# Fourteen expert tiles inside the last fourteen attention groups of a fused attention and mixture-of-experts block

## What is computed

```python
x = x + layernorm(attention(layernorm(x)))         # 16 heads of 16, causal, f16 weights
x = x + layernorm(moe(layernorm(x)))
...
logits = xt @ Ws + bs                              # 8 experts, two are taken for each row
topk_w, topk_idx = top_k(logits, 2); topk_w = softmax(topk_w)
h = silu(xt @ Wg[e]) * (xt @ Wu[e])                # F = 688
out = sum over the two experts e of topk_w * (h @ Wd[e])
```

## Time and profile before

| | us |
|---|---|
| median of 3 runs | 1003.47 (1001.80 to 1004.06) |
| profiled execution | 1003.02 |
| its span | 1001.3 |
| TensorE, VectorE, ScalarE, GpSimd busy | 824.3, 670.9, 549.9, 414.9 |
| TensorE clock granted, mean | 0.699 |

### The profile page before, as it was taken

The page is one execution under the profiler, slowest core; times in us unless marked ns, Lnnn a source line. Parts: engine busy times, 40 slices in busy tenths (PEclk is TensorE's granted clock), DMA queues, the critical chain, the costliest instruction groups (busy, mean ns, idle before and its releaser), DMA issues. The chain is left out here.

```text
span 1001.3 us, 22338 instructions
## 1 busy us (share of the span) xinstructions
PE 824.3 (82%) x6606; PEld 472.7 (47%) x6607; DVE 670.9 (67%) x2625; ACT 549.9 (55%) x1007; POOL 414.9 (41%) x428
## 2 busy tenths in 40 slices
PE   3488787799999999999982099999999999999800
PEld 1122232233333333333331087877877877877600
DVE  5667788888888988888864345555555555555535
ACT  4588877665565565556561044555555455455325
POOL 3565645562534534253445322333323323333316
PEclk9555555555555555555555599999999999999955
DMA  5344232228000101000011242323323323233164
GB/s 160 117 126 129 88 112 65 70 79 301 29 27 23 33 17 38 2 17 27 15 30 33 79 112 39 47 36 43 43 36 47 42 37 47 37 42 47 22 199 147
DMA packets 69219, 66.17 MB, mean 66 GB/s; under 512 B 5536, under 2 KB 62752, under 8 KB 69152
## 3 DMA queue, kind: packets, MB, share of 16 engines
q1 hardware_dynamic: 55872, 50.86, 16.7%
q0 software_dynamic: 13280, 14.49, 10.6%
HBM read 34.04 MB, written 31.29 MB: 65 GB/s over the span
## 5 line engine op out<-in xcount | busy, mean ns | idle before, releaser
L580 ACT ACTIVATE pT<-bank 128x512 f16<-128x512 f32 (+1 forms) x384 | 200.4, 530 | 161.9 <-PE bank L949 160.0
L691 DVE CUSTOM_DVE_ANT_0 unused<-bank,mask 128x384 f16<-128x384 f32 (+3 forms) x512 | 234.6, 483 | 73.9 <-PE bank L940 71.4
L1231 POOL DMA_INDIRECT expert_rows<-y_sb,dest x78 | 121.5, 1558 | 263.4 <-DVE y_sb L1350 224.1
L949 PE MATMUL bank<-qT,kT 32*128 32x384 f16 (+3 forms) x512 | 203.0, 449 | 23.8 <-ACT pT L580 23.6
L940 PE MATMUL bank<-kT,qT 32*128 32x384 f16 (+3 forms) x512 | 201.0, 446 | 16.8 <-DVE nmax L691 15.9
L1390 PE MATMUL bank<-xT,gu_part 128*128 128x256 f16 (+1 forms) x1716 | 202.7, 276 | 4.8 <-issue 3.8
L1390 PEld LDWEIGHTS bank<-xT,gu_part 128*128 (+1 forms) x1716 | 168.7, 100 | 36.8 <-issue 7.7
L1415 PE MATMUL bank<-wd_part,h 128*128 (+2 forms) x1326 | 163.6, 273 | 1.2 <-ACT h L1268 0.2
L482 POOL TENSOR_SCALAR_AFFINE_SELECT pT<-pT 128x512 f16<-128x512 f16 x128 | 79.8, 635 | 155.6 <-ACT pT L580 155.1
L1415 PEld LDWEIGHTS bank<-wd_part,h 128*128 128x128 f16 (+2 forms) x1326 | 117.2, 97 | 37.5 <-issue 24.5
L1268 ACT ACTIVATE h<-hid 128x512 f16<-128x512 f32 (+2 forms) x156 | 81.7, 523 | 89.0 <-DVE hid L1330 86.6
(11 more groups left out here) (150 smaller groups left out, 925.9 us busy)
## 6 DMA issues: line engine op xcount, KB each, us to landing
expert_rows<-clear SPq DMA_DIRECT2D x1, 8192.0 KB, 26.8
stage<-wg SPq DMA_DIRECT2D x8, 688.0 KB, 4.0
stage<-wu SPq DMA_DIRECT2D x8, 688.0 KB, 4.1
stage<-wd SPq DMA_DIRECT2D x8, 640.0 KB, 4.3
xin<-dispatch_rows SPq DMA_DIRECT2D x39, 130.0 KB
ys<-expert_rows SPq DMA_DIRECT2D x16, 256.0 KB, 6.0
out<-res SPq DMA_DIRECT2D x16, 256.0 KB, 2.1
x_sb<-x SPq DMA_DIRECT2D x8, 256.0 KB
```

The lines of the kernel that those rows point to most:

```text
L580: sc.activation(pT[:, lo:hi], ST_BANK[i % 2][:, 0:hi - lo], ACT.Exp, scale=1.0 / INV_SCALE).then_inc(p_ready, 1)
L691: last = v.tensor_tensor_reduce(out=unused[:, i % 2, at:at + n], in0=S_BANK[i % 2][:, at:at + n], in1=mask[:, T - n:T], scale=-1.0, scalar ...
L949: last = mm(ST_BANK[i % 2][:, at:at + n], kT[32 * j:32 * j + 32, g, P * kt:P * (kt + 1)], qT[32 * j:32 * j + 32, g, P * kt:T], start=True, ...
L1231: gp.indirect_dma_start(out=ys_dram[:, :], in_=y_sb[j][:, t, :], in_offset=None, out_offset=bass.IndirectOffsetOnAxis(ap=dest[j][:, t:t + ...
```

## The change

Fourteen of the 39 tiles (`EARLY_TILES`) are worked on inside groups 18 to 31 (`FIRST_TILE = 18`); `experts` keeps 25 (`LATER_TILES`). In each of these groups:

- TensorE does one of six chunks of gate and up products in each even step (`tile_up`, 8 products, the last chunk 4), one of six down chunks in steps 7, 9 and 11 and, for the tile of the group before, in steps 1, 3 and 5 (`tile_down`, 6 products, the last chunk 4), and transposes the next tile's rows in step 6. The gate and up chunk stands in one PSUM bank (`X_BANK`, the former `K_BANK`), gate in one half and up in the other, so `tile_up` waits for `hid_ready` of the chunk before. The down sums stand in the former `M_BANK`. All projections and transposes of attention share the remaining bank, one every second step.
- ScalarE takes tanh of half the gate in the even steps (`tanh`), makes high parts (`tile_high`) and takes the tile's result with the row's share (`take_tile_y`).
- VectorE computes silu times up in two operations at each odd step (`gate` and, at the step's end, `product`), and subtracts the low parts at fixed steps (`tile_low` at 6, 10, 11; `tile_last_low` at step 1 of the next group).
- GpSimd copies the rows' numbers and shares (`take_tile`) and issues the stores (`store_tile`, after the first cut of the next group; the last one after the last group).
- From sequence 3 on, VectorE plans which full tiles exist (`plan`, 17 small operations a sequence); SyncE loads them one group ahead.

Throughout attention `norm_centre` is gone: `norm_scale` subtracts the mean and multiplies in one operation, with the mean copied to f32 by GpSimd in `rsqrt`; the copies of y out of PSUM go from VectorE to ScalarE (`evict`); `x1` shares `y`'s memory. The table in `experts` starts each expert after the rows already done.

```diff
+FIRST_TILE = 4 * G + 2
+EARLY_TILES = G * B - FIRST_TILE
+LATER_TILES = TILES - EARLY_TILES
+CP = FC // 2
...
-        AT_Q, AT_K, AT_V, AT_MAXIMA = (1, 2), (3, 4), 5, (6, 7)
-        AT_ATT_T, AT_NEXT_T, AT_Y, AT_XN2_T = ((0, 7), (0, 8)), ((0, 10), (0, 11)), ((1, 0), (1, 2)), (2, 11)
-        AT_LOGITS, AT_RANKS = (3, 1), (3, 8)
+        EARLY_AT = ({"q": (1, 2), "k": (3, 4), "v": (5,), "max": (6, 7), "attT": (7, 8), "xnT": (10, 11)},
...
+                    {"q": (1, 2), "k": (3, 4), "v": (5,), "max": (6, 7), "logits": (1,), "ranks": (8,)})
+        TILE_AT = ({"q": (1,), "k": (3,), "v": (5,), "max": (7,), "attT": (9,), "xnT": (11,)},
...
+                   {"logits": (1,), "q": (3,), "k": (5,), "max": (7,), "ranks": (9,), "v": (11,)})
+        AT_TILE_T = 6
+        AT_UP = {2 * c: c for c in range(FC)}
+        AT_DOWN, AT_LATE_DOWN = {7: 0, 9: 1, 11: 2}, {1: 3, 3: 4, 5: 5}
...
+        HOME = {"q": 0, "max": 0, "k": 1, "y0": 1, "logits": 1, "ranks": 1, "v": 2, "attT": 2, "xnT": 2, "y1": 2,
+                "xn2T": 2}
+        TAIL_HOME = {"attT": 0, "y0": 1, "y1": 0, "xn2T": 0, "logits": 1, "ranks": 1}
...
+                def load_tile(n):
+                    sp.wait_ge(plan_ready, PLAN_OF[n] + 1)
+                    sp.wait_ge(keep["scattered"], 16 * TOP * QT * (PLAN_OF[n] + 2))
+                    if n:
+                        sp.wait_ge(tile_xT_mm, n)
+                        sp.wait_ge(tile_taken, n)
+                    else:
+                        sp.wait_ge(keep["cleared"], 16)
+                    row = sp.value_load(table[0:1, 0, n:n + 1], min_val=0, max_val=ROWS - TS)
+                    sp.dma_start(xin[:, :, :], xs_dram[bass.ds(row, TS), :].rearrange("(t p) d -> p t d", p=P)
+                                 ).then_inc(tile_in, 16)
...
                     gp.tensor_scalar(veps[:, :], mv[:, :, 1], LN_EPS16, None, ALU.add).then_inc(veps_ready, 1)
+                    gp.tensor_copy(mean[:, :], mv[:, :, 0]).then_inc(mean_ready, 1)
...
+                def take_tile(n):
+                    pool.wait_ge(tile_in, 16 * n + 16)
+                    if n >= 2:
+                        pool.wait_ge(tile_y_ready, n - 1)
+                        pool.wait_ge(keep["ys_early"], 32 * (n - 1))
+                    gp.tensor_copy(dest[n % 2][:, :], xin[:, :, :].bitcast(U32)[:, :, D // 2])
+                    gp.tensor_scalar(share[n % 2][:, :], xin[:, :, D // 2 + 1], 1.0 / (WSCALE * HSCALE), None, ALU.mult
+                                     ).then_inc(tile_taken, 1)
...
+                def store_tile(n):
+                    pool.wait_ge(tile_y_ready, n + 1)
+                    if n:
+                        pool.wait_ge(keep["ys_early"], 32 * n)
+                    else:
+                        pool.wait_ge(keep["cleared"], 16)
+                    for t in range(TS // P):
+                        gp.indirect_dma_start(
+                            out=ys_dram[:, :], in_=y_sb[:, t, :], in_offset=None,
+                            out_offset=bass.IndirectOffsetOnAxis(ap=dest[n % 2][:, t:t + 1], axis=0),
+                            compute_op=ALU.add,
+                        ).then_inc(keep["ys_early"], 16)
...
+                            if n >= 1 and c == 0:
+                                store_tile(n - 1)
+                            if n >= -1 and n + 1 < EARLY_TILES and c == 1:
+                                take_tile(n + 1)
...
+                store_tile(EARLY_TILES - 1)
...
+                def tanh(n, c):
+                    rows, cols = slice(0, P if c < FC - 1 else FR), slice(TS * (c % 2), TS * (c % 2) + TS)
+                    act.wait_ge(up_mm, FC * n + c + 1)
+                    if n == 0 and c == 0:
+                        act.wait_ge(lo_ready, PIECES)
+                    if n and c < FC - 1:
+                        act.wait_ge(h2_ready, CP * (n - 1) + c // 2 + 1)
+                    if n and c == FC - 1:
+                        act.wait_ge(low_ready, n)
+                    sc.activation(hid[rows, c // 2, cols], X_BANK[rows, 0:TS], ACT.Tanh, scale=0.5 / WSCALE
+                                  ).then_inc(tanh_ready, 1)
...
+                def tile_high(n, part):
+                    if n == 0 and part == 0:
+                        act.wait_ge(rows_cleared, 1)
+                    act.wait_ge(hid_ready, FC * n + (2, 4, 5, 6)[part])
+                    if n:
+                        act.wait_ge(down_mm, CP * (n - 1) + min(part, CP - 1) + 1)
+                    rows, m, cols = ((slice(0, P), 0, slice(0, 2 * TS)), (slice(0, P), 1, slice(0, 2 * TS)),
+                                     (slice(0, P), 2, slice(0, TS)), (slice(0, FR), 2, slice(TS, 2 * TS)))[part]
+                    sc.activation(h1[rows, m, cols], hid[rows, m, cols], ACT.Copy).then_inc(h1_ready, 1)
...
+                def take_tile_y(n):
+                    act.wait_ge(down_mm, CP * n + CP)
+                    act.wait_ge(tile_taken, n + 1)
+                    if n:
+                        act.wait_ge(keep["ys_early"], 32 * n)
+                    for t in range(TS // P):
+                        last = sc.activation(y_sb[:, t, :], Y_BANK[:, D * t:D * (t + 1)], ACT.Copy,
+                                             scale=share[n % 2][:, t:t + 1])
+                    last.then_inc(tile_y_ready, 1)
...
+                            if n >= 1 and i == 0:
+                                tile_high(n - 1, 3)
+                            if n >= 0 and i in (4, 8, 10):
+                                tile_high(n, (4, 8, 10).index(i))
+                            if n >= 0 and i in AT_UP:
+                                tanh(n, AT_UP[i])
...
-                def norm_centre(src, n, half):
+                def norm_scale(dst, src, n, half):
                     if half == 0:
-                        dve.wait_ge(var_ready, n + 1)
-                    for t in HALVES[half]:
-                        last = v.tensor_scalar(cen[:, t, :], src[:, t, :], mv[:, t, 0:1], None, ALU.subtract)
-                    if half:
-                        last.then_inc(cen_ready, 1)
-
-                def norm_scale(dst, n, half):
-                    if half == 0:
-                        dve.wait_ge(cen_ready, n + 1)
+                        dve.wait_ge(mean_ready, n + 1)
                         dve.wait_ge(rstd_ready, n + 1)
...
+                def gate(n, c):
+                    rows, cols = slice(0, P if c < FC - 1 else FR), slice(TS * (c % 2), TS * (c % 2) + TS)
+                    dve.wait_ge(tanh_ready, FC * n + c + 1)
+                    v.scalar_tensor_tensor(hid[rows, c // 2, cols], hid[rows, c // 2, cols], 1.0, X_BANK[rows, 0:TS],
+                                           ALU.add, ALU.mult).then_inc(gate_ready, 1)
+                def product(n, c):
+                    rows, cols = slice(0, P if c < FC - 1 else FR), slice(TS * (c % 2), TS * (c % 2) + TS)
+                    other = X_BANK[:, TS:2 * TS] if c < FC - 1 else X_BANK[P // 2:P // 2 + FR, 0:TS]
+                    dve.wait_ge(gate_ready, FC * n + c + 1)
+                    v.scalar_tensor_tensor(hid[rows, c // 2, cols], other, 0.5 * HSCALE / WSCALE / WSCALE,
+                                           hid[rows, c // 2, cols], ALU.mult, ALU.mult).then_inc(hid_ready, 1)
+                def tile_low(n, m):
+                    dve.wait_ge(h1_ready, 4 * n + m + 1)
+                    cols = slice(0, 2 * TS) if m < CP - 1 else slice(0, TS)
+                    v.tensor_tensor(h2[:, m, cols], hid[:, m, cols], h1[:, m, cols], ALU.subtract
+                                    ).then_inc(h2_ready, 1)
+                def tile_last_low(n):
+                    dve.wait_ge(h1_ready, 4 * n + 4)
+                    cols = slice(TS, 2 * TS)
...
+                            if n >= 1 and i == 1:
+                                tile_last_low(n - 1)
+                            if n >= 0 and i % 2:
+                                gate(n, i // 2)
+                            if n >= 0 and i in (6, 10, 11):
+                                tile_low(n, (6, 10, 11).index(i))
...
+                            if n >= 0 and i % 2:
+                                product(n, i // 2)
...
+                def tile_up(n, c, col):
+                    if c == 0:
+                        pe.wait_ge(tile_xT_out, n + 1)
+                    if n == 0 and c == 0:
+                        pe.wait_ge(k_taken, EARLY_USES[1])
+                    else:
+                        pe.wait_ge(hid_ready, FC * n + c)
+                    if c < FC - 1:
+                        sources = ((X_BANK[:, 0:TS], c * P, P), (X_BANK[:, TS:2 * TS], GU_UP + c * P, P))
+                    else:
+                        sources = ((X_BANK[0:UP_ROWS, 0:TS], GU_LAST, UP_ROWS),)
+                    for target, at, width_ in sources:
+                        for s in range(2 * KD):
+                            k, part = s // 2, s % 2
```

(13 more changed lines are left out.)

666 lines of the change are left out of this document (418 added, 248 removed), and 4 rows, old and new, of tables (EARLY_AT, TILE_AT).

## The result

| | before | changed |
|---|---|---|
| median, us | 1002.88 of 4 runs (1001.80 to 1004.06) | 1017.91 of 4 runs (1011.40 to 1021.47) |
| ratio | 1 | 1.0142, 95% interval 1.0085 to 1.0199 |
| profiled execution, its span | 1003.02, 1001.3 | 1020.0, 1018.2 |

The changed kernel is 1.4% slower. The forecast was 982 us and faster: the sign is wrong, though the time lies within the range of 950 to 1045 us.

The account below looks back on a forecast made before the run. TensorE was taken to bound attention (at half clock, VectorE close behind) and the expert stage. Tile groups +101.3, late clock +4.6, ends +8.3, first groups -2, experts -133.0: total -20.8, giving 982 us, range 950 to 1045 us.

Parts of the forecast that it names:

- I take the clock to rise within the first tile group and to stay: TensorE's clock in the tile groups: low for half a group, +4.6 us, then full to the end.
- rival R2: Tile groups: the clock rises and falls again, or rises late; half the groups at 31.3 us, 1042 us; chance 0.09.
- such a mixture: Tile groups: full-row tile products among 32-row scores, taken to resemble the stretch that raised the clock; no row showed it.
- The group, 22 us at full clock: Groups 18 to 29: each takes 22 us, from 18.0 loop, 3.0 odd-step work and 0.8 even-step work.
- Groups 30 and 31 ... 16.5 us each: Last two attention groups, without maxima: a loop of 2.4 to 2.7 us, 16.5 us each.
- the ring: Tile groups: two-step loop through one PSUM bank, TensorE's next chunk waiting for VectorE's product; 3.0 us, six times 18.0.
- Planning, "0.7 us per group at the 0.17 us of the short ones": VectorE in attention: about 17 short operations for three of four groups' batch add some 0.7 us per group.
- What stands in odd steps, between gate and product ..., lies on the loop ... about 3 us per group: Tile groups: VectorE's other work in odd steps, between gate and product or before the gate, adds about 3 us per group.
- The first 18 groups, -2: Attention ahead of the tiles: less VectorE work but bound by TensorE, between 0 and 5.5 us gained; -2 us taken.
- The ends, +8.3: After the last group: tile stores ahead of GpSimd's scatters and a copy more per rsqrt delay the last chain, +8.3 us.
- Expert stage, -133.0: Expert stage: fourteen tiles of 9.50 us leave it, -133.0 us.
- R3: Tile groups: no other VectorE work hidden, or other queues join the loop; 24 to 26 us, 1006 to 1030 us; chance 0.15.

Follow-up runs that it names:

- e10: Changed kernel with the second layer norm's scaling at steps 8 and 9 of the g = 2 groups instead of 9 and 10; 1023.7 us, ratio 1.0205.
- e2: Changed kernel plus two extra, unused TensorE products of 128 rows and 512 columns in every even step of the tile groups; 1018.0 us, ratio 1.0164.
- e3: Changed kernel plus the same extra products as e2, but of 32 rows; 1040.0 us, ratio 1.0389.
- e4: Changed kernel with the last tile's two stores issued behind the first root of the last sequence instead of ahead of the scatters; 1013.5 us, ratio 1.0092.
- e1: Changed kernel with VectorE's product right behind its gate instead of at the end of the odd step; 994.9 us, ratio 0.9927.
- e5: Changed kernel with the edits of e1 and e4 together; 989.6 us, ratio 0.9858.
- e8: e5 plus eight extra back-to-back products of 128 rows and 512 columns at the first step of group 18 alone; 988.2 us, ratio 0.9848.
- e11: e9 with e10's edit, the second norm's scaling a step earlier; 968.8 us, ratio 0.9675.
- e9: e6 with planning spread one or two operations to a step over ten steps, each settling the one before; 971.9 us, ratio 0.9681.
- e7: Changed kernel with the linked operations of the planning issued twice; 1031.9 us, ratio 1.0278.
- e12: e11 with y of the first four sequences copied out of PSUM by VectorE again; 969.8 us, ratio 0.9672.
- e6: e5 with gate and product also ahead of the maxima of their step on VectorE; 983.2 us, ratio 0.9813.

## Why the prediction was wrong, by its own steps

- **"I take the clock to rise within the first tile group and to stay"**: this step failed. It rose 22.4 us after the first tile product instead of half a group (15.7) and fell seven times for 61.4 us.

  What a microsecond at the lower clock costs: the interval of take_att 22 to 23 took 29.3 us with 20.5 low in the changed kernel, 25.9 with 10.2 in e10; that is 0.33, near the 0.30 of the text's (31.3 - 22) / 31.3 and the 0.29 between e2 and e3. Over the 14 intervals from take_att 17 to 31 of the changed kernel, e4 and e10, whose loops are the same but for one norm step, a straight line through the differences gives 0.32 (the same of e1, e5 and e8, with the shorter ring, 0.21). So 68 us more of it than forecast are an estimated 20 to 22 of the 29.8 us. By itself this step takes the forecast from 982 to some 1003 us, no change; the other terms below make it slower.

  This is rival R2, given 0.09; its price, 1042 us, assumed half the groups at the low clock (6.5 groups of 31.3 us, 203 us), three times what came. The choice rested on "such a mixture" being like the stretch of full-row products; attention in the earlier trace rows, with full-row projections and transposes among its scores, ran at 0.50 with TensorE 96% busy, and that row should have weighed more. The Trainium skill ("TensorE: Matmul & The Clock Gate", section "A second HAM failure mode") names short idle moments between groups of products as what makes the clock oscillate. Here it did oscillate beside pauses of up to 1.7 us, but e2, with nearly as much waiting (16.8 against 21.0 us), kept it up.
- **The group, 22 us at full clock**: right. Of the eleven intervals with maxima, take_att 17 to 28, five have no low clock and took 20.1, 23.6, 20.3, 21.7 and 19.6 us, mean 21.1; none of the five holds the planning. All eleven have a mean of 23.9 us, and an estimated 22.0 with 0.32 us taken off for each microsecond of low clock. In groups 18 to 29 the excess of 18.3 us over the forecast is by this estimate all clock: 63 us more of it at 0.29 to 0.33 give 18 to 21.
- **"Groups 30 and 31 ... 16.5 us each"**: mis-sized. They took 43.2 us together where 33 were forecast, with 6 us of low clock, worth about 2; some 8 us are left. Group 31, all at full clock, took 19.9 us, and in e11 both, at full clock, 19.3 and 18.1. The text dropped the maxima from the ring and took it to be 2.4 to 2.7 us for two steps. From 628 to 671.2 us VectorE's gate waited 11.8 us for ScalarE's tanh, for which no wait of note stands from 378 to 590 us. What held tanh back wasn't tried.

```profile
DVE stage L1066 <- ACT stage L742: 11.8, 9, 2.1
```

- **Planning, "0.7 us per group at the 0.17 us of the short ones"**: mis-sized. In the group shown its 15 operations (the text counts 17) took 4.3 us of VectorE in four pieces between 430.82 and 439.3 us, 0.29 us each, where four groups at 0.7 are 2.8; and spreading them gave 11.3 us (e9). The text priced the operations, not the wait of each for the one ahead, nor that two of the pieces stand in front of a product. Three of the 15 also lasted 0.58 to 0.65 us there.
- **"What stands in odd steps, between gate and product ..., lies on the loop ... about 3 us per group"**: right as a mechanism. At 3 us the twelve groups have 36 us of it; moving product ahead of it gave 23 us over all fourteen (e1), of which 37 us less of low clock are an estimated 8 to 12. The rest is about 1 us a group; what stands ahead of the gate stayed on the loop. That waits on the loop also bring the clock down was a rival (R2) and not in the sum.
- **The first 18 groups, -2**: wrong in sign, +6.9, and more than the 5 us that the text named as a sign of being wrong. Of these 2.4 are the planning in group 13 (e7, e9), 2.2 stand in the intervals of take_att 9 to 10, 11 to 12 and 13 to 14 (15.6, 15.8, 15.6 us before, 16.4 each after), 1.8 ahead of take_att 9. The last two are open: not the scaling's step (e10), not the copies of y (e12). A further 1.3 us stand in the rest of group 17, which has planning. The text allowed these groups no cost because TensorE bounds them. But VectorE's queue reaches TensorE there: its weight loads waited 9.5 us for maxima from take_att 9 to group 18 (223.3 to 341.1 us), where it was 6.4 us before.
- **The ends, +8.3**: +6.0 measured, by the mechanism named (e4): 53.0 - 47.0.
- **Expert stage, -133.0**: -131.7; the first tile, at the lower clock, took 7.70 us for its 44 products (6.49 before the change), where the earlier trace rows has 5.44 at full clock. (The 351.5 us of the earlier trace rows hold tiles 1 to 37, not 1 to 36 as the text says; its 351.5 / 37 is right.)
- R3 (no work hidden, 1006 to 1030 us) names the time that came, by luck: its full-clock groups of 24 to 26 us did not come.

## What to carry over

Where one buffer makes a ring through two engines, the release of that buffer goes right behind its last input, ahead of whatever the engine also has to do; here the place of one operation was worth 23 us. With the gate moved too and the last stores late, the same change is 1.9% faster than the kernel before (e6), and with the planning spread as well 3.3% (e11), instead of 1.4% slower. Price a chain of short dependent operations by the distance of their starts, and spread it. And a gain that hangs on a clock level has to be weighed as a case of its own as long as no row shows the clock holding that level over the same mixture of work.

## What was not expected of the hardware

With equal instructions, columns and places, extra products on 128 rows kept TensorE's clock up (15.8 us low in the tile groups), and on 32 rows they let it fall eight times (110.8 us). One of them lasted 378 to 379 ns in both where the clock was up, and TensorE was busy 90% and 92% of the stretch, so it isn't TensorE's busy share that told them apart. And waits of TensorE up to 1.6 us long did not bring the clock down by themselves: e2 waited 16.8 us for the product and its clock fell once from 378 to 590 us; e3 waited 11.7 us, and it fell five times.
